# A decoder's mixed attention: output projections three blocks later, key slots cleared by GpSimd, context products behind the first searches, first largest scores sent by ScalarE

## The reference, cut to what matters

```python
x = _layernorm(x + _L0_attn_ref(x, ...))            # linear attention
x = _layernorm(x + _L0_xattn_ref(x, ctx_512, ...))  # mixed attention: here
x = _layernorm(x + _L0_ffn_ref(x, ...))             # experts
x = _layernorm(x + _L1_attn_ref(x, ...))            # state space
x = _layernorm(x + _L1_xattn_ref(x, ctx_512, ...))  # block attention, "a1" and "a2"
x = _layernorm(x + _L1_ffn_ref(x, ...))

def _L0_xattn_ref(x, ctx, ...):                     # 16 heads of 16, per batch
    y = softmax(causal(q(x) @ k(x).T)) @ v(x) + softmax(cq(x) @ ck(ctx).T) @ cv(ctx)
    return y @ Wp + bp
```

## Time and profile before

| | us |
|---|---|
| runs of the kernel | 4046.64, 4058.03, 4063.96 |
| median | 4058.03 |
| the profiled execution, whole | 4045.47 |
| its span, first to last instruction | 4044.2 |
| mixed attention in it | about 174 to 1305 |

### The profile page before, as it was taken

How to read it: one execution, slowest core, us unless ns; L and a number is a source line. 1 busy time by engine, 2 the same in 40 slices (tenths; PEclk the granted TensorE clock), 3 DMA queues, 4 the chain that set the end, 5 groups by cost and what they waited for, 6 DMA issues and landing times. The chain is left out here.

```text
span 4044.2 us, 59055 instructions
## 1 busy us (share of the span) xinstructions
PE 3511.0 (87%) x22156; PEld 2135.3 (53%) x22156; DVE 2255.6 (56%) x4065; ACT 1681.3 (42%) x3067; POOL 983.5 (24%) x1030
## 2 busy tenths in 40 slices
PE   6779999999999884788877689999999996899998
PEld 3433443444443772444546545555555545787877
DVE  6747667577573337544426567676676624534432
ACT  1125646556456231333434135545555553322222
POOL 1200100000000103233333335555555462200000
PEclk9868989999899996898989789999999997999999
DMA  1011211212110311353322244443443402122211
GB/s 68 12 39 45 63 36 45 60 45 51 49 44 23 143 62 42 56 77 62 59 46 76 48 58 63 62 65 56 65 60 58 61 14 77 49 84 63 64 59 61
DMA packets 144627, 229.42 MB, mean 57 GB/s; under 512 B 40916, under 2 KB 90840, under 8 KB 141400
## 3 DMA queue, kind: packets, MB, share of 16 engines
q1 hardware_dynamic: 129048, 216.21, 25.4%
q10 hardware_dynamic: 15296, 9.45, 1.2%
HBM read 99.39 MB, written 8.91 MB: 27 GB/s over the span
## 5 line engine op out<-in xcount | busy, mean ns | idle before, releaser
L940 DVE TENSOR_REDUCE a_mp<-bank 128x1 f32<-128x384 f32 (+2 forms) x1280 | 704.7, 592 | 443.9 <-PE bank L790 429.8
L898 ACT ACTIVATE a_p<-bank 128x512 f32<-128x512 f32 (+1 forms) x1088 | 594.8, 595 | 595.5 <-PE bank L815 523.4
L898 ACT ACTIVATE mx_p<-bank 128x512 f32<-128x512 f32 (+3 forms) x1088 | 548.9, 557 | 471.2 <-PE bank L815 256.2
L940 DVE TENSOR_REDUCE mx_mp<-bank 128x2 f32<-128x768 f32 (+4 forms) x640 | 596.6, 956 | 233.7 <-PE bank L790 143.0
L976 POOL TENSOR_TENSOR a_pair<-a_p 128x512 f32<-128x512 f32 x384 | 491.4, 1310 | 462.0 <-ACT a_p L898 462.0
L790 PE MATMUL bank<-a_ks,a_qs 126*128 126x384 f32 (+2 forms) x1280 | 438.9, 410 | 63.8 <-issue 26.3
L815 PE MATMUL bank<-a_qs,a_ks 128*128 128x512 f32 (+1 forms) x1088 | 421.9, 452 | 41.4 <-DMA a_qs<-a_mt 20.5
L815 PE MATMUL bank<-mx_qs,mx_ks 64*128 64x512 f32 (+3 forms) x1088 | 344.7, 477 | 21.0 <-DMA mx_qs<-mx_mt 13.4
L790 PEld LDWEIGHTS bank<-a_ks,a_qs 126*128 126x128 f32 x1280 | 248.9, 196 | 215.7 <-issue 108.1
L201 POOL TENSOR_TENSOR rs<-ve,neghalf 128x4 f32<-128x4 f32 (+2 forms) x80 | 78.0, 976 | 1168.2 <-DVE ve L196 1125.2
L790 PE MATMUL bank<-mx_ks,mx_qs 62*128 62x384 f32 (+4 forms) x1280 | 314.2, 429 | 7.4 <-DVE mx_mp L940 6.8
(11 more groups left out here) (311 smaller groups left out, 5580.1 us busy)
## 6 DMA issues: line engine op xcount, KB each, us to landing
sf_raw<-in_h_w SPq DMA_DIRECT2D x64, 512.0 KB, 3.5
a_ks<-a_kh SPq DMA_DIRECT2D x96, 192.0 KB, 4.5
ex_w<-in_L_ffn_w SPq DMA_DIRECT2D x16, 1024.0 KB, 5.0
a_qs<-a_qh SPq DMA_DIRECT2D x64, 256.0 KB, 6.1
mx_ks<-mx_kh SPq DMA_DIRECT2D x192, 48.0 KB, 2.1
a_ks<-a_kl SPq DMA_DIRECT2D x48, 192.0 KB, 5.2
mx_qs<-mx_qh SPq DMA_DIRECT2D x128, 64.0 KB, 2.2
mx_rec<-mx_flat SPq DMA_DIRECT2D x128, 64.0 KB, 2.0
```

The source lines that it names most:

```text
L898: act.activation(probs[place % len(probs)][0:kp, q0:T], self.bank(part, n, kb, h)[0:kp, q0:T], ACT.Exp, scale=scale).then_inc(*self.frees( ...
L940: v.tensor_reduce(best[:, tiled * j:tiled * j + tiled, i, ci], bank[:, 0:w] if tiled == 1 else bank[:, :, 0:w], AX.X, ALU.max).then_inc(*s ...
```

## The change

- `attention_steps` gets a list `behind`; what it holds is written after the first searches (and `steady`, which narrows the ring of banks that beside groups take, moves behind it). In the mixed attention the seven context products and their load are moved there from `during`. The block attention passes an empty list.
- Key slots 1 and up are all cleared by POOL; DVE clears slot 0 alone. This holds for the block attention too.
- For the eight jobs of batch 0 the largest scores are copied and sent by ACT, with ACT's own DMAs, and no longer by DVE and SP.
- `finish` steps 1 to 4 stand beside blocks 10 to 13 of the next batch, the moments at 16, the norm at 19.

```diff
-        yield "steady",
         while found < total[0]:
             yield from peaks(found + 8, 8, True)
...
         yield from split(True)
+        for group in behind:
+            yield from side(group)
+        yield "steady",
...
-        def slot_made(i):
-            eng, name = ((v, "k_slots_made_dve"), (g, "k_slots_made_pool"))[i % 2]
...
+        def k_slot_made(i, eng):
+            name = "k_slots_made" if i else "k_slot_made"
...
             for i in range(1, k_slots):
-                slot_made(i)
+                k_slot_made(i, g)
...
+        tops_by_act = lambda n: summed or jobs[n].b == 0
...
-            elif part == "tops_turned" and summed:
+            elif part == "tops_turned" and tops_by_act(n):
...
-                    sp.wait_ge(*has(("k_slots_made_dve", "k_slots_made_pool")[slot % 2], slot, tiled - 1))
+                    sp.wait_ge(*has("k_slots_made" if slot else "k_slot_made", slot))
...
-                    beside[begin + 7 + i].append([("finish", b - 1, 1 + i)])
-                at_once[begin + 13].append([("finish", b - 1, TB + 1)])
-                at_once[begin + 16].append([("finish", b - 1, TB + 2)])
+                    beside[begin + 10 + i].append([("finish", b - 1, 1 + i)])
+                at_once[begin + 16].append([("finish", b - 1, TB + 1)])
+                at_once[begin + 19].append([("finish", b - 1, TB + 2)])
...
-            [[("own", 0, i)] for i in range(KC, KC + TB)] + [[("context", 0, i)] for i in range(VG + 1)], beside, at_once, [[("finish", NB - 1, i)] for i in range(TB + 3)], 2.6, 4, 13)
+            [[("own", 0, i)] for i in range(KC, KC + TB)], [[("context", 0, i)] for i in range(VG + 1)], beside, at_once, [[("finish", NB - 1, i)] for i in range(TB + 3)], 2.6, 4, 13)
```

More of the change, by code:

```diff
@@ L509, in linear_attention, with attention_steps @@
             pool_part(b, *part)
-    def attention_steps(self, jobs, q_slots, k_slots, tiled, before, during, beside, at_once, after, rate, lead, urgent):
+    def attention_steps(self, jobs, q_slots, k_slots, tiled, before, during, behind, beside, at_once, after, rate, lead, urgent):
         blocks = [(n, kb) for n, job in enumerate(jobs) for kb in range(-(-job.nk // P))]
@@ L684, in softmax_attention @@
         qst = [sb(f"qs{i}", [P, HT, T], F32R) for i in range(q_slots)]
-        def slot_made(i):
-            eng, name = ((v, "k_slots_made_dve"), (g, "k_slots_made_pool"))[i % 2]
-            for r, at in enumerate(base):
+        def k_slot_made(i, eng):
+            name = "k_slots_made" if i else "k_slot_made"
+            for at in base:
                 row = 3 * D // 32 * 32 + at
-                eng.memset(kst[i][row:at + full].bitcast(F32), -1.0).then_inc(*up(name, i, r))
-                eng.wait_ge(*has(name, i, r))
+                eng.memset(kst[i][row:at + full].bitcast(F32), -1.0).then_inc(*up(name, i))
+                eng.wait_ge(*has(name, i))
         def q_slot_made(i, eng):
@@ L915, in act_part @@
                 act.activation(turned[:, :], self.bank("turn_tops", n)[0:2 * HG, :], ACT.Copy).then_inc(*self.frees("turn_tops", n))
-            if summed and part in ("tops_turned", "gather", "flat", "spread"):
+            if part == "tops_turned" and tops_by_act(n) or summed and part in ("gather", "flat", "spread"):
                 small_transfer(act, part, n)
@@ L953, in dve_part @@
                                 ).then_inc(*up("tops_made", n))
-            elif part == "tops_turned" and not summed:
+            elif part == "tops_turned" and not tops_by_act(n):
                 if n:
@@ L1037, in sp_part @@
                 k_order.append((n, at[0]))
-            elif not summed:
+            elif part == "tops_turned" and not tops_by_act(n) or not summed and part in ("gather", "flat", "spread"):
                 small_transfer(sp, part, n)
@@ L1874, in block_attention @@
         q_slots, k_slots, tiled = 3, 7 if cross else 5, 1
-        order = lambda: self.attention_steps(jobs, q_slots, k_slots, tiled, before, during, beside, at_once,
+        order = lambda: self.attention_steps(jobs, q_slots, k_slots, tiled, before, during, [], beside, at_once,
                                              whole(finish_of(NB - 1, *range(5))), 5.2 if cross else 4.2, 3, 9)
```

2 lines of the change are left out of this document (1 added, 1 removed).

## The result

| | before | changed |
|---|---|---|
| median of 20 runs, us | 4052.14 | 4059.43 |
| lowest and highest | 4032.37 to 4064.46 | 4041.95 to 4071.12 |
| the profiled execution, whole | 4045.47 | 4041.95 |
| last block of the mixed attention begins | 1303.98 | 1306.99 |

What follows compares the result with a forecast made beforehand. PE, busy 87% of the span, was taken as the bound, losing time to waits and half clock. -5.4 - 1.5 - 3.0 - 1.0 + 0.5 + 1.6 = -8.8 us from 4058.0 gave 4049; 8-in-10 range 4022 to 4066.

Steps and rivals of the forecast that it cites:

- The start: Start of the mixed attention: first weigh at 211.2 for 216.58, -5.4 us; up to two blocks behind it at full clock, -1.5.
- Job 1: Batch 0: ACT's sending of the largest scores avoids SP's queue, shortening PE's 6.45 us from turn to weigh, -3.0 us.
- ACT's load: Batch 0: each of eight sendings puts 1.9 us ahead of ACT's exps; +0.5 us, 0 to +4.
- The waits for the copies: Batch 0: a few of PE's eleven waits for DVE's copy of the largest scores go, -1.0 us (0 to -2.5).
- Projections: Three later batches, blocks 7 to 10: waits for mx_y go, but half clock lasts until the first projection in block 10; +1.6 us.
- The bound for this part in the range, +3: Upper end of the likeliest case's range: +3 us for the projections standing three blocks later.
- Cost it the same; within 1 us: Moments and norm, three blocks later on DVE, were to cost the same, within 1 us.
- (a): Later batches: the wait for mx_y holds the clock down, so blocks 7 to 10 run full; total -28.6 us, 4029, chance 0.25.
- (b): Later batches: the second projection, not the first in block 10, brings the clock back; 11.1 us more, 4060, chance 0.17.
- (c): Later batches: the low clock lasts until the cross jobs at block 16; total +36 us, 4094, chance 0.08.
- (d): Stage start: cold context products and DVE's adds leave -2.1 for -5.4, no clock gained; 4054, within the likeliest case's range.

Runs made afterwards that it cites:

- second profile: The changed kernel run once more with no edit: median 4057.3 us, ratio 1.0004 to the kernel before.
- start and ACT: The changed kernel with projections, moments and norm back at blocks 7, 13 and 16: median 4050.1 us, ratio 0.9989 to the kernel before.
- the better kernel: The changed kernel with ACT sending for batch 0's self jobs alone, projections at 8, 9, 10, 13, moments 14, norm 17: 4034.0 us, ratio 0.9959.

## Why the prediction was wrong

The sign was wrong: -8.8 us forecast, +7 by the medians, +10 by the ratio. The time itself, 4059.4, lies in the range, but that is no merit of the sum, which was reckoned from 4058.0, the median of three runs of the kernel before, where twenty give 4052.1. Step by step:

- **The start, -5.4 and -1.5.** Right: -5.1 to the first weigh, -1.2 in blocks 0 and 1. The terms in it were right only together: 7.65 us for the context products where 9 were taken, and a wait of 0.8 us for DVE that was not seen. That POOL's clearing alone might give as much or more was missed: what the products cost behind a dense stretch, 5.78 us, was not asked.
- **Job 1, -3.0.** -2.6 measured.
- **ACT's load, +0.5.** Mis-sized: +3.8 in blocks 26 to 29 and block 52 (+5.3 in the second profile), for an upper bound of 4. The step "ACT is busy 98 of 225 us there, so it has room" failed. Room on the mean doesn't help where the copy comes between two exps that PE waits for. The waits for the copies, -1.0 forecast, gave nothing: three of them fall in batch 0 (210 to 480 us), 2.5 us before with DVE's copy and 3.3 with ACT's.
- **Projections, +1.6: the step that failed.** The part up to the first projection was right: the clock fell in block 5, with PE busy 5.07 of 5.12 us, it came back in block 10, and blocks 7 to 10 took 20.4, 20.8 and 20.1 us, for 21.2 forecast. The failing sentence is "The other three come later at full clock, 3 x 1.99 = 6.0". Blocks 11 to 13 grew by 10.4, 10.6 and 8.3 us where these three projections were priced at 6.0: a second fall of the clock, one more slow projection (+1.5 to +1.8), a wait for the turned scores (+1.1 to +1.3) and half clock around them. That is +9 us on the sum, which turns +1.6 into the +10.6 of the two profiles. The bound for this part in the range, +3, stood there without a working. By the ratios, which take in how the clock falls from run to run, moving the projections costs 6 us, with the rest of the change (1.0004 for 0.9989 in the same set of runs) and without it (1.0014).
- **What stood behind block 13.** "Cost it the same; within 1 us" for moments and norm missed 0.6 us in each block 16 (4.03 us, 3.41 before), 1.9 in all. And the sum compared a forecast with one profile of before, whose clock happened not to fall in block 13. With the projections at 7 to 10 such a fall comes in ten of 18 batches.
- **Rivals.** (a) fell: with the wait gone the clock was low all the same, and eight added products ended the spell. In blocks 14 and 15 the clock stood at 0.50 with PE busy all 8.32 us, and at 1.00 with 0.7 us of waits once a projection stood in block 13; it fell in block 5 with PE busy 5.07 of 5.12 us. The Trainium skill, "TensorE: Matmul & The Clock Gate", section "HAM oscillation — how this bites in real kernels", has the clock lost in idle gaps. The trace disagrees for these stretches; for the falls around block 13, which had 1.0 to 2.1 us of waits ahead of them, it leaves it open. (b) was nearest in size, with another mechanism: not the second projection but the third was slow. (c) did not come, nor (d): the start gained its 5.1 us.

By the ratios the parts alone make -6 (start), -4.5 (start and ACT) and +5.7 (projections), so about +1 together; the changed kernel measured +10 and then +1.6. Their intervals overlap, and the rest can't be told apart from scatter.

## What to carry to other kernels

In this kernel wide products were also what brought TensorE's clock back: in 40 of 42 batches the low spell of block 5 ended with a group of them, and eight added ones ended it where nothing else was moved. So try them where the profile shows the clock low in narrow work, and don't judge their place by the wait in front of them: one of four projections, moved by two blocks into a stretch of narrow products, took 12.4 us off 39 blocks in one profile of each kernel, and the better kernel is 17 us (10 to 23) under the one before. Ask of each moved step what stands right ahead of it in its new place (here a turn, whose copy on DVE it had to wait for). And when a stretch's time depends on the clock, read it in every batch of several profiles before taking a difference.

## What the runs showed of the hardware that was not expected

- The same order on PE took 52.5 to 63.8 us for 13 blocks in one profile, by where the clock fell (mean clock 0.93 and 0.68). PE at half clock can be fully busy (8.32 of 8.32 us), so idle time doesn't show the loss.
- The low spell of block 5 came in all 42 batches of the fourteen profiles, in narrow work (62- and 64-row products, values with 17 columns of weights) with 0.4 us of idle time in the 5 us ahead of it. In 40 of them it ended in a group of 128x128 products or within 1.3 us behind one, wherever that stood (block 7, 8 or 10); in the other two the clock rose 0.1 and 0.2 us ahead of the first projection in block 10. In 6 of the 18 batches with projections from block 7 on the first group didn't do it, and the second did.
- The low spells that began around block 13 ended in a projection in that block or up to 2.4 us behind it, where one stood there; else they lasted 14 to 24 us. With a projection in block 13, blocks 14 and 15 ran at 1.00 in 18 batches of 18; without one they ran at 0.50 in 14 of 24.
- 26 context products took 5.8 us behind the own value products with the slots cleared by POOL (two profiles), and 7.0 to 7.7 behind searches and the turn (ten profiles).
